# Seven more tiles of the second block in seven products, and the inverse root one step earlier, in a gated feed-forward kernel

## What is computed

```
scale = cond @ norm_w.T + 1.0
ms = jnp.mean(x * x, axis=-1, keepdims=True)
h = x * (scale[:, None, :] * jax.lax.rsqrt(ms + EPS))
u = h @ up_w.T
val, gate = jnp.split(u, 2, axis=-1)
h = val * jax.nn.gelu(gate, approximate=False)
hq = act_quant(h)          # per row, 8 bits
wq = weight_quant(down_w)  # three values and one scale
y = hq @ wq.T
return y + x
```

## Time and profile before

| | |
|---|---|
| median of 3 runs | 738.48 us (738.23 to 739.54) |
| profiled execution | 738.35 us |
| its span | 736.6 us |
| TensorE busy in it | 726.2 us (99%) |
| VectorE busy | 530.1 us (72%) |
| ScalarE busy | 344.0 us (47%) |
| GpSimd busy | 247.1 us (34%) |

### The profile page before, as it was taken

How to read it: one execution, slowest core, us unless ns; L and a number is a source line. 1 busy time by engine, 2 the same in 40 slices (tenths; PEclk the granted TensorE clock), 3 DMA queues, 4 the chain that set the end, 5 groups by cost and what they waited for, 6 DMA issues and landing times.

```text
span 736.6 us, 14962 instructions
## 1 busy us (share of the span) xinstructions
PE 726.2 (99%) x5722; PEld 558.4 (76%) x5722; DVE 530.1 (72%) x1024; ACT 344.0 (47%) x680; POOL 247.1 (34%) x341
## 2 busy tenths in 40 slices
PE   7999999999999999999999999999999999999998
PEld 6544444444688887888888888888888888888874
DVE  5567777976889665786668866788558875677457
ACT  5789766442355532346234543445434443344330
POOL 1211477777234700353005511155013530033100
PEclk9999999999999999999999999999999999999999
DMA  8877583747645454434344435444264323273202
GB/s 329 294 275 237 183 279 134 270 162 255 203 158 158 144 158 151 133 130 129 121 143 164 140 104 177 132 142 145 66 211 135 103 88 124 77 247 100 70 29 85
DMA packets 44567, 117.63 MB, mean 160 GB/s; under 512 B 5584, under 2 KB 5840, under 8 KB 43344
## 3 DMA queue, kind: packets, MB, share of 16 engines
q1 hardware_dynamic: 44496, 116.68, 48.0%
HBM read 99.88 MB, written 16.79 MB: 158 GB/s over the span
## 4 chain that ended last, share of the span: by engine, by line
PE 95%; DVE 2%; issue 1%; DMA 0%; POOL 0%; ACT 0%; DVEq 0%; SPq 0%; POOLq 0%
PE ps_v L656 14%; PE ps_v L658 14%; PE ps_v L657 14%; PE ps_y L792 7%; PE ps_g L658 6%; PE ps_g L657 6%; PE ps_g L656 6%; PE ps_y L785 5%; PE ps_v L674 4%; PE ps_g L674 4%; PE ps_g L676 4%; PE ps_v L676 4%; PE ps_v L675 4%; PE ps_g L675 4%; PE ps_v L914 1%
## 5 line engine op out<-in xcount | busy, mean ns | idle before, releaser
L656 PE MATMUL ps_v<-x_hi,w_hi 128*128 128x256 f16 x968 | 263.9, 273 | 1.5 <-DVE ps_v L1307 1.5
L658 PE MATMUL ps_v<-x_hi,w_lo 128*128 128x256 f16 x968 | 263.9, 273 | 0.0
L657 PE MATMUL ps_v<-x_lo,w_hi 128*128 128x256 f16 x968 | 263.8, 273 | 0.0
L933 ACT COPY ps_g<-ps_v 128x256 f32<-128x256 f32 x96 | 34.3, 357 | 196.9 <-PE ps_v L658 196.5
L949 ACT ACTIVATE g<-ps_g,w_unscale 128x512 f32<-128x512 f32 x128 | 87.4, 683 | 70.2 <-PE ps_g L658 65.9
L956 ACT ACTIVATE g<-h 128x512 f32<-128x512 f32 x128 | 81.4, 636 | 58.0 <-DVE h L1319 58.0
L656 PE MATMUL ps_g<-x_hi,w_hi 128*128 128x256 f16 x392 | 106.8, 273 | 0.1
L657 PE MATMUL ps_g<-x_lo,w_hi 128*128 128x256 f16 x392 | 106.8, 273 | 0.0
L658 PE MATMUL ps_g<-x_hi,w_lo 128*128 128x256 f16 x392 | 106.8, 273 | 0.0
L1171 POOL TENSOR_TENSOR sums<-q 128x256 f16<-128x256 f16 (+1 forms) x40 | 40.1, 1002 | 196.4 <-DVE q L1404 196.4
L656 PEld LDWEIGHTS ps_v<-x_hi,w_hi 128*128 128x128 f16 x968 | 94.7, 98 | 14.2 <-DVE ps_v L1307 2.3
(11 more groups left out here) (153 smaller groups left out, 1153.7 us busy)
## 6 DMA issues: line engine op xcount, KB each, us to landing
w_lo<-w_lo_dram SPq DMA_DIRECT2D x96, 448.0 KB, 3.2
q<-in_up_t_dram SPq DMA_DIRECT2D x16, 512.0 KB, 4.8
xt<-in_x_cols_dram SPq DMA_DIRECT2D x8, 1024.0 KB, 6.3
res<-in_x_rows_dram SPq DMA_DIRECT2D x26, 256.0 KB, 4.1
out_dram<-res SPq DMA_DIRECT2D x26, 256.0 KB, 4.1
xs<-in_x_rows_dram SPq DMA_DIRECT2D x22, 256.0 KB, 3.4
w_lo_dram<-w_lo SPq DMA_DIRECT2D x16, 256.0 KB, 4.3
dw<-in_down_t_dram SPq DMA_DIRECT2D x8, 512.0 KB, 6.4
```

The costliest lines, as they stand in the source:

```text
L656: pe.matmul(to, w_hi[:, wh:wh + P], hi, start=start and kt == 0, stop=False, skip_group_check=True)
L657: pe.matmul(to, w_hi[:, wh:wh + P], lo, start=False, stop=False, skip_group_check=True)
L658: last = pe.matmul(to, w_lo[:, wl:wl + P], hi, start=False, stop=(kt == 1), skip_group_check=True)
```

## The change

- Steps 25 to 31 (tiles 9 to 15 of block 1) are made in seven products; before, the first was step 32. Block 1 therefore gets the operands that tiles in seven need (4 differences, and 4 more high and low parts), made in block 0 by the new tables `T_FIRST`, `HIGH_FIRST`, `LOW_FIRST`.
- The 16 weight sums are made in steps 20 to 35 without gaps, in the order of tiles 9 to 15, 0 to 8 (before: 0 to 15, in steps 20 to 28, 30 to 33, 36 to 38). The loads stand 2 steps ahead throughout.
- The bursts of differences and low parts of blocks 2 and 3 are spread over steps by `T_EARLY`, `HIGH_EARLY`, `LOW_EARLY`. In block 1 quantized tiles come three at a time at first.
- The root of blocks 4 to 7 stands in step 13 of its block in place of 14, and two low parts (XB21, XB22) in step 15 in place of 13 and 14. The root of block 3 stays in step 30, that of block 2 in step 14.
- `down(0, 0)` stands at the end of step 31 in place of the middle of step 32, where it covered the first copies; `direct_second(24)` now covers those of step 25. Two places in `x_hi` and `x_lo` move, and the load of block 2's columns waits for seven low parts of block 1 where it waited for four.

```diff
-    SUM_AT = (20, 21, 22, 23, 24, 25, 26, 27, 28, 30, 31, 32, 33, 36, 37, 38)
+    FIRST = 9
+    N7 = J + FIRST
+
+    SUM_TILE = [*range(FIRST, J), *range(FIRST)]
+    SUM_AT = range(20, 36)
-    SUM_AHEAD = (2, 2, 1) + (2,) * 10 + (4, 4, 4)
+    SUM_AHEAD = (2, 2, 1) + (2,) * 13
...
-        return n >= 2 * J
+        return n >= N7
...
+        if c == 1:
+            return (XB11, XB12, XB21, XB22, XT1, XT2, XT3, XN4)
...
+    Q_COUNT_FIRST = (3, 3, 2, 2, 2, 2, 1, 1)
...
-    LOW_AT = {XB11: 9, XT1: 10, XT2: 12, XT3: 13, XB21: 13, XB22: 14, XN4: 15}
-    HIGH_EARLY = {XB11: 2, XT1: 2, XT2: 2, XT3: 2, XB21: 3, XB22: 3, XN4: 3}
+    LOW_AT = {XB11: 9, XT1: 10, XT2: 12, XT3: 13, XB21: 15, XB22: 15, XN4: 15}
+    T_EARLY = {XT1: 3, XT2: 5, XT3: 8, XN4: 11}
+    HIGH_EARLY = {XB11: 3, XT1: 4, XT2: 6, XT3: 9, XB21: 9, XB22: 10, XN4: 12}
+    LOW_EARLY = {XB11: 4, XT1: 8, XT2: 12, XT3: 13, XB21: 14, XB22: 15, XN4: 15}
+    T_FIRST = {XT1: 10, XT2: 10, XT3: 11, XN4: 13}
+    HIGH_FIRST = {XB11: 8, XB12: 8, XB21: 9, XB22: 9, XT1: 11, XT2: 11, XT3: 12, XN4: 14}
+    LOW_FIRST = {XB11: 9, XB12: 9, XB21: 11, XB22: 12, XT1: 12, XT2: 13, XT3: 13, XN4: 15}
...
-            return {1: 5, 2: 14, 3: J + 14}.get(c, (c - 2) * J + 14)
+            return {1: 5, 2: 14, 3: J + 14}.get(c, (c - 2) * J + 13)
...
-                    sp.wait_ge(x_lo_ready, made_before(c) - (1 if c >= 3 else 0))
+                    sp.wait_ge(x_lo_ready, made_before(c) - (1 if c >= 2 else 0))
...
-                if n == 2 * J:
-                    down(b - 2, 0)
+                if n == N7:
+                    direct_second(n - 1)
...
-                if n < NJ and not seven:
+                if n + 1 < N7:
                     direct_second(n)
...
-                if b >= 1 and b - 1 not in D_SEVEN and j == J - 1 and n + 1 != 2 * J:
+                if b >= 1 and b - 1 not in D_SEVEN and j == J - 1:
                     down(b - 1, 0)
...
-                    if j == 10:
-                        low(1, XB11)
-                        low(1, XB12)
-                    if j == 12:
-                        low(1, XB21)
-                        low(1, XB22)
+                    for k in (XT1, XT2, XT3, XN4):
+                        if j == T_FIRST[k]:
+                            difference(1, k)
...
-                if 1 <= b < 3:
-                    if j == 2:
-                        difference(b + 1, XT1)
-                        difference(b + 1, XT2)
-                        low(b + 1, XB11)
-                        difference(b + 1, XT3)
-                        low(b + 1, XT1)
-                        difference(b + 1, XN4)
-                    if j == 15:
-                        for k in (XT2, XT3, XB21, XB22, XN4):
-                            low(b + 1, k)
-                if 3 <= b < NB - 1:
+                for k in made(1):
+                    if n == LOW_FIRST[k]:
+                        low(1, k)
+                if 1 <= b < NB - 1:
                     for k in (XT1, XT2, XT3, XN4):
-                        if j == T_AT[k]:
+                        if j == (T_EARLY if b < 3 else T_AT)[k]:
                             difference(b + 1, k)
```

More of the change, by code:

```diff
@@ L416, in x_part, with halves, slot @@
         def x_part(parts, c, k):
[L419 to L424, removed]
+            def halves(at):
+                return parts[:, at:at + 2 * TB].rearrange("p (a n) -> p a n", a=2)
+            def slot(half, place):
+                at = (half * NOP + place) * 2 * HB
+                return parts[:, at:at + 2 * HB].rearrange("p (a n) -> p a n", a=2)
+            if k == XN4:
+                return slot(0, 6) if c % 2 == 1 else halves(XO)[:, :, HB:TB]
+            if c < 2 and k in (XB11, XB12, XB21, XB22):
+                first = 0 if k in (XB11, XB21) else HB
+                return halves(c * XO + (0 if k in (XB11, XB12) else 2 * TB))[:, :, first:first + HB]
+            if c % 2 == 0:
+                return slot(0, k)
+            if k == XB11:
+                return halves(XO)[:, :, 0:HB]
+            return slot(1, {XB21: 2, XB22: 3, XT1: 4, XT2: 5, XT3: 6}[k])
         def wb(j):
@@ L475, in store_sum @@
                 sp.wait_ge(ws_ready, k + 1)
-                sp.dma_start(lo_dram[k][:, WA:WL], sum_tile(k)).then_inc(stored, 16)
+                sp.dma_start(lo_dram[SUM_TILE[k]][:, WA:WL], sum_tile(k)).then_inc(stored, 16)
             def load_lo(n):
@@ L485, in load_lo @@
                     if n < 3 * J:
-                        stored, count = sum_store(j)
+                        stored, count = sum_store(SUM_POS[j])
                         sp.wait_ge(stored, count)
@@ L1006, in sum_high @@
             def sum_high(k):
+                j = SUM_TILE[k]
                 act.wait_ge(s_step, 4 * (k + 1))
[L1008 to L1010 removed]
+                act.wait_ge(val_ready, (J if j + 1 < FIRST else 0) + min(j + 2, J))
+                act.activation(w_hi[:, wb(j) + WA - PAD:wb(j) + WO].rearrange("p (a n) -> p a n", a=2), sum_raw(k), ACT.Copy,
+                               scale=w_scale[:, j:j + 1]).then_inc(ws_hi_ready, 1)
             def sum_down(k):
@@ L1052, in _ @@
                 if b == 0:
-                    if j == 9:
-                        high(1, XB11)
-                        high(1, XB12)
-                    if j == 10:
-                        high(1, XB21)
-                        high(1, XB22)
+                    for k in made(1):
+                        if j == HIGH_FIRST[k]:
+                            high(1, k)
                 for k in range(J):
@@ L1271, in difference @@
             def difference(c, k):
-                before = (c - 2) * 4
+                before = (c - 1) * 4
                 if k == XT1:
@@ L1489, in _ @@
                 tiles = []
-                if 1 <= b < NB and 0 <= k < len(Q_COUNT):
-                    tiles = Q_ORDER[sum(Q_COUNT[:k]):sum(Q_COUNT[:k + 1])]
+                count = Q_COUNT if b > 1 else Q_COUNT_FIRST
+                if 1 <= b < NB and 0 <= k < len(count):
+                    tiles = Q_ORDER[sum(count[:k]):sum(count[:k + 1])]
                 for t in tiles:
```

24 lines of the change are left out of this document (11 added, 13 removed).

## The result

| | before | the change |
|---|---|---|
| median of the runs | 738.48 us | 745.63 us (744.91 to 746.41) |
| ratio of the times | | 1.0096, 95% interval 1.0084 to 1.0108 |
| profiled execution | 738.35 us | 745.63 us |
| its span | 736.6 us | 743.8 us |

The change is slower by 7.15 us. The forecast was 739.2 us and the range ended at 742.8: the time is outside it, beyond rival B too.

The account below looks back on a forecast made before the run. TensorE, busy 99% of the span, was taken as the bound, with VectorE at its limit in block 0. Terms -4.2 - 1.5 + 2.5 + 3.9 = +0.7 us on the profiled 738.35, plus 0.13, gave 739.2 us; range 735.5 to 742.8.

Parts of the forecast that it names:

- rival B: VectorE bounds steps 12 to 15 and 26 to 31, it and GpSimd lengthening each other: +4.6, 743.1 us; chance 0.33.
- Term 1: Block 1, TensorE: seven tiles lose columns by going from eight products to seven, 0.60 us each: -4.2 us.
- rival C: TensorE: matmuls of 256 columns cost more than half of one of 512; time 745 us, chance under 0.01.
- Term 2: Root moved to step 13 of its block: the three TensorE waits of 0.49 us for `second_val` go, -1.5 us.
- Term 3: Block 0: VectorE's four added differences and four low parts delay tiles 13 to 16 on TensorE, +2.5 us.
- Term 4: Block 1: late VectorE and block 3's root in step 30 make TensorE wait for `second_val` in step 31, +3.9 us.
- the forecast's 0.37: Whole kernel: no measurable change, within about 0.2% or 1.5 us of the time before; chance 0.37.

Follow-up runs that it names:

- e12_low_first: The changed kernel with the low part ahead of the weight sum's low part in steps 20, 24 and 28 to 31: 742.55 us.
- e5_small_sums: The changed kernel with GpSimd's part of weight sums 7 to 15 made on 2 of 256 columns, leaving out most additions: 739.23 us.

## Why the prediction was wrong

**Term 1 (-4.2) held.** Where TensorE doesn't wait, a step in seven takes 4.58 us in the change as in the earlier trace rows, and rival C didn't happen. The seeds of steps 26 to 29, forecast 4.6 to 5 us apart, came 4.44, 4.38, 4.85 and 5.67 us behind the one before: VectorE's lateness starts later and grows faster.

**Term 2 (-1.5) was undersized: -2.0 to -2.1.** The three waits of 0.49 went, as predicted; each cost 0.16 more than is listed, as the waits of the change do: 3 x 0.65.

**Term 3 (+2.5) measured +3.1.** VectorE's scales of tiles 13 to 15 start at 83.64, 89.95 and 96.47, 6.3 and 6.5 us apart where TensorE's tile takes 5.24. The total came out near, in part by luck, because the waits stand elsewhere than the prediction said. Of 2.5 us listed, only 1.0 is for `w_lo`, 1.5 for the next tile's weight peak: behind the late scale (written from 84.22 on) ScalarE makes the high weights (84.41) and then the next peak (85.46), GpSimd clamps it (86.68), and TensorE goes on at 87.07.

**Term 4 (+3.9) is the step that failed: +9.1** (4.9 + 4.2). Against its own working:

- Missed: VectorE's wait ahead of `sum_low`, 0.58 us for ScalarE's high part in steps 27, 29 and 30. In step 28 it is 0.74, and the trace names a DMA there, the store that empties `xs`. The prediction counted VectorE's instructions and one wait of 0.36, and not this second one, of which the earlier trace rows show 0.48. It is ScalarE's own order (absolute value, gelu, then the sum's cast, which starts too late). By e12_low_first it holds about 2.2 of the waits' 6.6 us.

```profile
170.27 1.40 DVE L1252 SCALAR_TENSOR_TENSOR xs<-dw,w_scale,w_hi 128x1024 f16<-128x1024 f32 x1 [0.74 <-DMA w_lo_dram<-xs]
```

- Too low: a low part 1.14 instead of 0.95, the root 4.43 instead of 3.6. Both bounds were known from the earlier trace rows; I took values between because GpSimd "pauses", and beside this root it sits idle for 0.69 us only, ahead of 185.80. Together: the work behind the seed of step 30 was priced at 5.95 us, and takes 180.50 to 188.08 = 7.6.
- So VectorE's last steps before the root cost 5.4 to 5.7 us and not 4.6 to 5: two small waits before the large one, 6.6 in all.
- Not foreseen at all: the clock after a long wait, 1.7 us. The term was priced as if TensorE went on at its old pace.

The wait behind the root was placed rightly (step 31, `second_val`, 189.21 instead of "near 183") and sized 5.2 against 3.9. **Rival B was the larger part of what happened.** e5_small_sums shows it: without GpSimd's work the waits for `second_val` fall from 6.6 to 2.4 us and block 1 is 5.7 us shorter, the clock's 1.7 among them. ScalarE's wait, which B doesn't have, is the other part. That B's bound for term 4 (6.5) and the waits (6.6) are so near is partly luck, since the bound held 5.0 for the root and nothing for ScalarE. The range ended at 742.8, under B's own 743.1; what carries the change past both is the clock's 1.7 and, in the time but not in the blocks, the 1.16 us of the start.

The Trainium skill, SBUF — State Buffer, section Who interferes with whom, says that a VectorE instruction with two inputs in SBUF contends with a GpSimd instruction that reads SBUF. The trace agrees: the low part goes from 1.14 to 0.61 with GpSimd at rest, `hidden` stays at 0.74 to 0.75. Two rows of the root with one SBUF input (L1265, L1270) lengthen as well, 0.69 and 0.57 against 0.16 and 0.17; no run shows by which way.

The forecast took the middle of both terms as independent, although both rest on the same durations with GpSimd working. Rival B, at 0.33, deserved more than the forecast's 0.37.

**Open:** 0.3 us of block 1 in the change; which of the two or three operands added in steps 10 to 12 makes the weight peaks late in block 0; and whether GpSimd's work matters there too, since e5_small_sums leaves block 0 as it is.

## What to carry to other kernels

When tiles become cheaper on the bounding engine, the next engine's whole step is due sooner: add up its step with every wait for a third engine in it, at the durations it has while its neighbour works, before pricing the one large item. Put a long serial chain where the bounding engine has work that doesn't need you (here under a down projection), and fill a short wait for another engine with an instruction that is ready. Test table edits alone: the part that gained (the root in step 13) was hidden under the part that lost.
